# A transformer layer's first stage: deriving the combined weights inside the product loop, and moving row statistics to ScalarE

## What is computed

```python
xn = _layernorm(x, axis=-1)                       # (x - mean) / sqrt(var + 1e-5)
qkv = einsum('bsc,cf->bsf', xn, Wqkv) + bqkv      # 3 x 512 columns
attn = softmax(q @ k.T / sqrt(512)) @ v;  attn = attn @ Wo + bo
q_r = einsum('bsd,rd->bsr', xn, Wq_w)             # router, 16 columns
scores = einsum('bsr,er->bse', q_r, keys)         # 64 experts, the top 16 kept, softmax over them
z = einsum('bsd,nd->bsn', xn, A_w) * gate         # 512 columns
x = x + attn + einsum('bsn,on->bso', z, B_w) * 2
```

## Time and profile before

| | |
|---|---|
| Time, median of 3 runs | 2958.62 us (2958.13 to 2960.61) |
| Profiled execution: its own time, span | 2959.48 us, 2957.6 us |
| PE, PEld busy, share of the span | 94%, 76% |
| DVE, ACT, POOL busy | 63%, 32%, 25% |
| Mean granted PE clock | 0.983 |
| Phase A, groups 0 to 3: first matmul of the group at | 41.4, 442.6, 779.2, 1114.7 us |

### The profile page before, as it was taken

One profiled execution on the slowest core, in us unless ns is written; L12 is line 12 of the kernel. 1 busy time (PEld: TensorE's weight loads), 2 busy tenths in 40 slices (PEclk: granted clock), 3 DMA queues, 4 the chain that ended last, 5 costly groups with the idle time before them and its releaser, 6 DMA issues.

```text
span 2957.6 us, 34124 instructions
## 1 busy us (share of the span) xinstructions
PE 2772.5 (94%) x12096; PEld 2249.8 (76%) x12096; DVE 1858.8 (63%) x2133; ACT 931.8 (32%) x1164; POOL 736.4 (25%) x429
## 2 busy tenths in 40 slices
PE   2888999999999999999889999999999999999999
PEld 1666787878778787888668788787887878878787
DVE  5876777666776777364466655666556665566653
ACT  1222232323232223322244333343433434334331
POOL 7165212030120203020030502305033050330521
PEclk8999999999999999999999999999999999999999
DMA  9767455544554454333533534535445353453544
GB/s 371 232 234 237 153 192 166 183 138 152 187 180 142 163 177 137 115 99 107 180 105 121 174 131 137 178 121 174 130 136 177 122 176 128 136 176 124 175 143 136
DMA packets 261611, 476.34 MB, mean 161 GB/s; under 512 B 26864, under 2 KB 76016, under 8 KB 257264
## 3 DMA queue, kind: packets, MB, share of 16 engines
q1 hardware_dynamic: 223408, 372.45, 39.0%
q10 hardware_dynamic: 29376, 68.72, 6.6%
q0 software_dynamic: 8704, 33.56, 3.2%
HBM read 390.74 MB, written 83.91 MB: 160 GB/s over the span
## 4 chain that ended last, share of the span: by engine, by line
PE 74%; DVE 11%; DMA 4%; issue 4%; ACT 3%; SPq 2%; POOL 2%; DVEq 0%; ACTq 0%; POOLq 0%
PE psum L689 31%; PE psum L1448 13%; PE psum L1450 13%; PE psum L1449 13%; DVE prob L1645 3%; DVE w_lo L739 2%; PE psum L626 2%; DVE r_lo L1617 1%; ACT r_hi L1338 1%; SPq L362 1%; DVE s_lo L744 1%; DVE part L726 1%; DMA t_scratch<-xb 1%; DMA w_raw<-t_scratch 1%; DMA xb<-W_blocks 1%
## 5 line engine op out<-in xcount | busy, mean ns | idle before, releaser
L739 DVE TENSOR_TENSOR w_lo<-w_raw,w_hi 128x1024 fp32r<-128x1024 f32 x224 | 325.7, 1454 | 417.0 <-ACT w_hi L442 416.6
L442 ACT ACTIVATE w_hi<-w_raw 128x1024 fp32r<-128x1024 f32 x224 | 237.4, 1060 | 946.4 <-PE psum L689 812.7
L1617 DVE TENSOR_TENSOR r_lo<-r_raw,r_hi 128x1024 fp32r<-128x1024 f32 x256 | 380.3, 1500 | 189.4 <-ACT r_hi L1338 189.4
L1448 PE MATMUL psum<-r_hi,f_hi 128*128 128x512 f32 x1024 | 405.7, 396 | 30.4 <-DVE r_lo L1617 29.0
L1449 PE MATMUL psum<-r_lo,f_hi 128*128 128x512 f32 x1024 | 400.8, 391 | 0.0
L1450 PE MATMUL psum<-r_hi,f_lo 128*128 128x512 f32 x1024 | 400.6, 391 | 0.0
L689 PE MATMUL psum<-s_hi,w_hi 128*128 128x512 f32 x896 | 356.3, 398 | 40.8 <-DVE w_lo L739 27.6
L1583 POOL TENSOR_TENSOR res<-res,b_out 128x512 f32<-128x512 f32 x128 | 222.8, 1769 | 661.4 <-DMA res<-x 661.4
L689 PE MATMUL psum<-w_hi,s_hi 128*128 128x512 f32 x896 | 353.8, 395 | 32.5 <-DVE w_lo L739 32.4
L689 PE MATMUL psum<-s_lo,w_hi 128*128 128x512 f32 x896 | 352.9, 394 | 0.0
L689 PE MATMUL psum<-s_hi,w_lo 128*128 128x512 f32 x896 | 352.5, 393 | 0.0
(11 more groups left out here) (133 smaller groups left out, 4287.0 us busy)
## 6 DMA issues: line engine op xcount, KB each, us to landing
w_raw<-t_scratch SPq DMA_DIRECT2D x128, 512.0 KB, 3.9
w_raw<-W_blocks SPq DMA_DIRECT2D x96, 512.0 KB, 3.9
r_raw<-k_scratch SPq DMA_DIRECT2D x64, 512.0 KB, 3.8
r_raw<-v_scratch SPq DMA_DIRECT2D x64, 512.0 KB, 4.6
r_raw<-B_T SPq DMA_DIRECT2D x64, 512.0 KB, 3.9
res<-x SPq DMA_DIRECT2D x128, 256.0 KB, 4.9
r_raw<-Wo SPq DMA_DIRECT2D x64, 512.0 KB, 4.5
out<-res SPq DMA_DIRECT2D x128, 256.0 KB, 3.4
```

The costliest lines, as they stand in the source:

```text
L442: nc.scalar.activation(w_hi[:, s % RAW], w_raw[:, s % RAW], ACT.Copy).then_inc(s_whi, 1)
L739: nc.vector.tensor_tensor(w_lo[:, s % RAW], w_raw[:, s % RAW], w_hi[:, s % RAW].bitcast(F32), ALU.subtract).then_inc(s_wlo, 1)
L1448: pe.matmul(bank, sh, mh, start=first, stop=False)
L1617: nc.vector.tensor_tensor(r_lo[:, slot, :], r_raw[:, slot, :], r_hi[:, slot, :].bitcast(F32), ALU.subtract).then_inc(b_lo, 1)
```

## The change

Five things change together, nearly all in the first group.

1. **Weight sums on the way.** `sums_t` and its 1 MB loads are gone. In products 2 to 5 of the first group, DVE subtracts right after it has split a step's weights (`sum_weights`): it takes the raw weights that lie in `w_raw` and one more block that POOL has loaded. b22 (the weights of product 2) less b12 gives t3; b21 less b11 (this subtraction on POOL, `less_b11`) less t3 gives t4; b21 less t4 gives t2; b22 less t2 gives t1. SP stores each 512 KB result to `t_scratch` behind its weight load, and the next product loads it from there. The extra blocks lie in four slots of x12's place (products 2 and 3), then in `rows`.
2. **Rows first.** At the start ACT issues the four row tiles and then x11; SP issues the constants, and holds the first two weight loads back until row tiles 1 and 3 have landed. x21 and x22 are loaded by POOL, after the first two pairs of x11 are split.
3. **Router weight in rows.** `WqT` is laid out on the host so that a partition's 256 values are contiguous (before: runs of 16). Its split moves ahead of the loop.
4. **Statistics of later tiles on ACT** (`moments`): two passes over 128 x 2048 with the sum as a second output (Identity, then Square with the mean as bias) and three operations on one column. This is for tiles 4, 6 and 7 of the first group, at (0,3), (0,5), (0,6), and for all tiles of the next group at the new `STATS_AT`. Tile 5 stays on DVE, at (0,4). `store_stats` moves from (0,5) to (0,7), `broadcast_stats` from (0,6) to (1,0).
5. **Normalisation.** The pairs of x21 and x22 are at (1,1) to (1,4), two in each step; before they were spread over (1,0) to (1,4). Those of the second group's x12 are at (4,3) to (4,6) instead of (4,1), (4,2), (4,3), (4,5).

```diff
+SUMMED = {2: "t3", 3: "t4", 4: "t2", 5: "t1"}
 BIAS = [[4, 5, 0, 1], [6, 7, 2, 3]]
-STATS_AT = [(1, 1), (1, 2), (1, 3), (1, 4), (2, 1), (2, 2), (2, 3), (3, 1)]
+STATS_AT = [(1, 1), (1, 2), (1, 5), (2, 1), (2, 2), (2, 3), (2, 5), (2, 6)]
...
+NORM1_AT = [(4, 3), (4, 4), (4, 5), (4, 6), (5, 1), (5, 2), (5, 3), (5, 5), (6, 1), (6, 2), (6, 3), (6, 6)]
+OWN_AT = {(0, 3): 4, (0, 5): 6, (0, 6): 7}
...
+    def t_tile(idx, s):
+
+        return x_pair(1, s % PART) if idx < 4 else row_tile(s)
+
+    def row_tile(s):
+        return rows[:, s % PART // 2, s % 2 * 2 * W:(s % 2 + 1) * 2 * W].rearrange("p (a w) -> p a w", w=W)
...
-            if static(g) and g == 0 and ORDER[idx][1] in W_SUM:
-                for h in (s * 2, s * 2 + 1):
-                    sp.wait_ge(s_tstore[t_slot(h)], 16 * t_uses(t_slot(h), h + 1))
+            if static(g) and g == 0:
+                i, k = (idx, s - RAW) if s >= RAW else (idx - 1, s - RAW + IPI)
+                if i in SUMMED:
+                    sp.wait_ge(s_tdiff, t_number(i, k))
+                if idx - 1 in SUMMED:
+                    sp.wait_ge(s_tstore[s % PART], 16 * t_uses(idx - 1, s))
             sp.dma_start(w_raw[:, s % RAW], w_source(idx, s)).then_inc(s_raw[s % RAW], 16)
...
-            sp.dma_start(wq_raw[:], WqT.rearrange("(k p) r -> p k r", p=P)).then_inc(s_const, 16)
+            sp.dma_start(wq_raw[:].rearrange("p k r -> p (k r)"), WqT).then_inc(s_const, 16)
...
+        constants()
+        sp.wait_ge(s_row0[1], 16)
         load_w(0, 0, 0)
-        for p in range(PART):
-            sp.dma_start(x_pair(0, p), xT[2 * p * P:(2 * p + 2) * P, 0:W].rearrange("(a p) t -> p a t", p=P)
-                         ).then_inc(s_x[0][p], 16)
+        sp.wait_ge(s_row0[HT - 1], 16)
         load_w(0, 0, 1)
...
+                    if static(g) and g == 0 and idx in SUMMED:
+                        sp.wait_ge(s_tdiff, t_number(idx, s))
+                        sp.dma_start(t_block(idx, s), t_tile(idx, s)).then_inc(s_tstore[s % PART], 16)
...
+        def moments(g, j):
+            tile = rows[:, j % 2, :]
+            col = slice(j, j + 1)
+            if static(g) and g == 0:
+                base, loads = max(j - HT - 1, 0) * STAT_STEPS, (j - HT) // 2 + 1
+            else:
+                base, loads = (g * NTOK - NTOK + len(OWN_AT) + j) * STAT_STEPS, g * HT - HT // 2 + j // 2 + 1
+            chain = Chain(act, s_moments, base)
+            act.wait_ge(s_rows[j % 2], 16 * loads)
+            chain.link(nc.scalar.activation(tile, tile, ACT.Identity, accum_out=total[:, col]))
+            chain.step(nc.scalar.activation(mv[:, 0, col], total[:, col], ACT.Copy, scale=1.0 / C))
+            chain.link(nc.scalar.activation(less_mean[:, col], total[:, col], ACT.Copy, scale=-1.0 / C))
+            chain.link(nc.scalar.activation(tile, tile, ACT.Square, bias=less_mean[:, col], accum_out=squares[:, col]))
+            chain.link(nc.scalar.activation(var[:, col], squares[:, col], ACT.Copy, scale=1.0 / C))
+            act.sem_inc(s_amv, 1)
...
+        for p in range(PART):
+            x_load(0, 0, p)
+        act.wait_ge(s_const, 64)
+        act.wait_ge(s_wq, 1)
+        nc.scalar.activation(wq[:, :, 0:RD], wq_raw[:], ACT.Copy).then_inc(s_wq, 1)
...
+                    if first and (idx, s) in OWN_AT:
+                        moments(0, OWN_AT[idx, s])
...
+                        if s == 6:
                             square_roots(2, slice(HT, NTOK))
-                            wait(act, s_tiles, HT)
-                            for p in range(PART):
-                                x_load(0, 3, p)
-                        if s == 5:
+                        if s == 7:
                             store_stats(0, 2, HT)
-                        if s == 6:
-                            broadcast_stats(0, 2, HT)
+                    if first and idx == 1 and s == 0:
+                        broadcast_stats(0, 2, HT)
...
+                        if (idx, s) in STATS_AT:
+                            j = STATS_AT.index((idx, s))
+                            moments(g + 1, j)
+                            if j + 2 < NTOK:
+                                rows_load(g + 1, j + 2)
...
+        def sum_weights(idx, s):
+            tile = t_tile(idx, s)
+            dve.wait_ge(s_tload[s % PART], 16 * (t_uses(idx, s) + 1))
+            if idx == 3:
+                dve.wait_ge(s_tsum, s + 1)
+            if idx == 2:
+                ins = nc.vector.tensor_tensor(tile, w_raw[:, s % RAW], tile, ALU.subtract)
+            else:
+                ins = nc.vector.tensor_tensor(tile, tile, w_raw[:, s % RAW], ALU.subtract)
+            ins.then_inc(s_tdiff, 1)
...
+                    after = (idx, s + 1) if s + 1 < IPI else (idx + 1, 0)
+                    if first and after[0] in SUMMED:
+                        sum_weights(*after)
...
-                        if s < HT:
-                            stats_of_tile(0, HT + s)
                         if s == 3:
                             norm_pair(0, 1, 0)
                         if s == 4:
-                            rstd_ready(NTOK, slice(HT, NTOK))
-                            norm_pair(0, 1, 1)
-                            rstd_finish(2, NTOK * TILE_STEPS + RSTD_STEPS, slice(HT, NTOK))
-                        if s in (5, 6):
+                            stats_of_tile(HT + 1)
+                        if 4 <= s <= 6:
                             norm_pair(0, 1, s - 3)
+                        if s == 6:
+                            dve.wait_ge(s_mv, HT + 1)
+                            rstd_ready(len(OWN_AT), slice(HT, NTOK))
+                        if s == 7:
+                            rstd_finish(2, (HT + 1) * TILE_STEPS + RSTD_STEPS, slice(HT, NTOK))
                     elif first and idx == 1:
-                        if s == 0:
-                            norm_pair(0, 2, 0)
-                        if 1 <= s <= 3:
+                        if 1 <= s <= 4:
+                            norm_pair(0, 2, s - 1)
...
-        def sums_t(h):
-            slot, p, k = t_slot(h), h // HK, h % HK
-            b = t_tile(slot)
-            b11, b12, b21, b22 = (b[:, i, :] for i in range(4))
-            pool.wait_ge(s_tload[slot], 16 * t_uses(slot, h + 1))
-            nc.gpsimd.tensor_tensor(b11, b12, b11, ALU.subtract).then_inc(s_tadd, 1)
-            pool.wait_ge(s_tadd, 4 * h + 1)
-            nc.gpsimd.tensor_tensor(b12, b22, b12, ALU.subtract).then_inc(s_tadd, 1)
-            pool.wait_ge(s_tadd, 4 * h + 2)
-            nc.gpsimd.tensor_tensor(b22, b22, b11, ALU.subtract).then_inc(s_tadd, 1)
-            pool.wait_ge(s_tadd, 4 * h + 3)
-            nc.gpsimd.tensor_tensor(b21, b21, b22, ALU.subtract).then_inc(s_tadd, 1)
-            pool.wait_ge(s_tadd, 4 * h + 4)
-            pool.dma_start(t_scr[:, p, k * P:(k + 1) * P, :].rearrange("b p w -> p b w"), b
-                           ).then_inc(s_tstore[slot], 16)
...
+        def load_b12(s):
+            if s < PART:
+                pool.wait_ge(s_slo, pair(0, 2, s) + 1)
+            else:
+                stored(2, s - PART)
+            load_summand(2, s, "b12")
+
+        def load_b21_b11(s):
+            stored(2, PART + s) if s < PART else stored(3, s - PART)
+            load_summand(3, s, "b21")
+            if s < 2:
+                pool.wait_ge(s_amv, len(OWN_AT) + NTOK)
+            if s >= PART:
+                pool.wait_ge(s_tsum, s - PART + 1)
+            pool.dma_start(row_tile(s), w_block("b11", s // PART, s % PART)).then_inc(s_tload1[s % PART], 16)
+
+        def less_b11(s):
+            pool.wait_ge(s_tload[s % PART], 16 * (t_uses(3, s) + 1))
+            pool.wait_ge(s_tload1[s % PART], 16 * (s // PART + 2))
+            nc.gpsimd.tensor_tensor(t_tile(3, s), t_tile(3, s), row_tile(s), ALU.subtract).then_inc(s_tsum, 1)
+
+        def load_b21(s):
+            if s < PART:
+                pool.wait_ge(s_tsum, PART + s + 1)
+            else:
+                stored(4, s - PART)
+            load_summand(4, s, "b21")
+
+        def load_b22(s):
+            stored(4, PART + s) if s < PART else stored(5, s - PART)
+            load_summand(5, s, "b22")
...
+        pool.wait_ge(s_slo, 2)
+        for p in range(PART):
+            for block in (2, 3):
+                if block == 3:
+                    pool.wait_ge(s_tiles, HT)
+                pool.dma_start(x_pair(block, p), xT[((block % 2) * HK + 2 * p) * P:((block % 2) * HK + 2 * p + 2) * P, W:TG]
+                               .rearrange("(a p) t -> p a t", p=P)).then_inc((s_tload1, s_tload)[block - 2][p], 16)
         for p in range(PART):
             s3(0, p)
             s4(0, p)
-        sums_t(7)
-        load_t(9)
-        sums_t(8)
-        load_t(10)
-        sums_t(9)
-        load_t(11)
-        for h in range(10, T_ITEMS):
-            sums_t(h)
-            if h + 2 < T_ITEMS:
-                load_t(h + 2)
-        for p in range(PART):
-            s2_s1(0, p)
+        for s in range(IPI):
```

(13 more changed lines are left out.)

177 lines of the change are left out of this document (85 added, 92 removed).

## The result

The changed kernel takes 2951.12 us (median of 11; 2942.82 to 2955.75), the kernel before on the same chip 2960.61 (median of 11). The ratio is 0.9966, 95% interval 0.9956 to 0.9976: faster by 0.34%. The forecast was 2932, and its range ended at 2951. The sign was right and the size was a third of the forecast: 9.5 us instead of 27. The last digits of such a difference carry little: with no edit in groups 1 and 2, these two together took 1.6 to 3.6 us longer in every experiment's trace than in the changed kernel's.

What follows compares the result with a forecast made beforehand. PE's idle bounds it: about 118 us up to the end of product 4. Start and products 0 to 4 sum to 324.5 against 354.4, 29.9 less; less 0.8 and 2, 27.1 off 2959.5 gives 2932; range 2903 to 2951.

Steps and rivals of the forecast that it cites:

- Start, product 0: First matmul at 30 us instead of 41.4; product 0 takes 51 us, the 20.5 us wait for `wq` gone.
- the term of four tiles: Start: four row tiles of 3.3 us plus 0.8 for the router weight's split; the last starts at 15.7.
- ACT's statistics: Two passes of 2.0 us each, 5.0 a tile; groups 1 and 2 lose 2 us for both.
- rival 2: Crowded queues and slow ACT: 7 us a tile, 9 in all, product 2 stays at 52; 2945 to 2953; chance 0.18.
- Product 1: 84 us instead of 73.4: statistics in place at 21.4, then steps of 13.1 as DVE and POOL take turns.
- Product 3: 61 us, as now: 48 plus 13 for b11, the chain, the statistics store and queues; bounds 50 and 75.
- the wait for b11: Start of product 3: DVE stands for POOL's first b11 subtraction (9.5 us), delaying the split for (3,1); PE loses 3 us.
- the chain: Product 3: store landing, issues and subtractions bind each second tile, 11.5 us for two steps; costs 2 us.
- the store of the statistics: Product 3: the store at (3,4), landing in 10.2 us, holds up what is issued behind it; costs 6.6 us.
- Product 4: 50 us, 2 more than now: new subtraction and pair in (4,4), s2 and s1 turns in first three steps.
- Rival 3: Chain through HBM binds: landings of 11.0 us, 20 more in product 3, 15 in products 2, 4, 5; 2967; chance 0.06.
- Rival 1: Most idle goes (store lands in half the time or DVE and POOL overlap): 2907, 2893 at its end; chance 0.22.

Runs made afterwards that it cites:

- e9: Changed kernel with the router weight fetched in short runs as before, still first on SP's queue: 2965.37 us in one execution.
- e5: Changed kernel with POOL's block differences of product 1, first group, cut to 32 columns (outputs differ): 2936.49 us in one execution.
- e11: e8 with the x differences of product 1, first group, on DVE instead of POOL: 2929.17 us, ratio 0.9877.
- e7: e4 with three places on DVE reordered: subtraction of (3,0) behind drains, router copy of (3,3) earlier, x12 pairs one step later: 2948.42 us, ratio 0.9939.
- e6: e4 with group 1's statistics earlier on ACT and POOL's b11 subtraction ahead of its load for tile s+2: 2942.98 us, ratio 0.9920.
- e15: Changed kernel with only the eight subtractions of b11 moved from POOL to DVE: 2950.50 us in one execution.
- e14: Changed kernel with only POOL's arithmetic of the first group moved to DVE: 2932.78 us, ratio 0.9885.
- e4: Changed kernel with the broadcast of group 1's statistics issued at (4,0) instead of (3,5): 2950.22 us, ratio 0.9945.
- e16: e12 with the store of group 1's statistics in 32-byte instead of 4-byte runs (second group's statistics go to wrong tokens): 2912.56 us in one execution.
- e12: e11 with all of POOL's other arithmetic of the first group on DVE too: 2919.59 us, ratio 0.9844.
- e13: e12 with the store of group 1's statistics at (2,5) instead of (3,4): 2918.85 us, ratio 0.9842.
- e8: Changed kernel with the edits of e4, e6 and e7 together: 2937.65 us, ratio 0.9904.

## Why the prediction was right in sign and wrong in size

*Start, product 0: right.* First matmul at 31.2, no wait for `wq`, product 0 52.3. The second to fourth tiles come at DVE's pace (10.80, 13.97 and 17.14), as the term of four tiles assumed, and 14.1 us lie behind the last (forecast 14). e9 shows how much hangs on it: without the router weight in rows all is lost. It also corrects the reading of the earlier trace rows: the short runs hold SP 7.3 us by themselves, not 35.4.

*ACT's statistics: right.* The two passes take 1.9 and 2.01 us, and their accumulator reads 0.18 each, in all 4.7 a tile (forecast 5.0). Groups 1 and 2 moved by less than 0.5 us instead of 2. The first half of rival 2 (7 us a tile) is out, and so is its second: product 2 takes 45.4.

*Product 1: right in its steps, and by some luck in its sum.* Steps of 12.3 us (forecast 13.1). e5 and e11 confirm the turns in two independent ways: 62.7 us with POOL's part made small, 9.7 us a step with it on DVE. The rule of the Trainium skill (SBUF — State Buffer, section SBUF: two separate sides), that a DVE instruction with two SBUF inputs and a GpSimd one that reads SBUF exclude each other, is borne out. That (1,0) to (1,2) take 32.2 us, as forecast, is luck: the broadcast landed in 10.2 us, not 5.3, the store in 8.3, not 12.3, and the long pause came before (1,3), not before (1,2).

*Product 3: this step failed.* It read: "3 us of PE" for the wait for b11, "with the other work of DVE it costs 2" for the chain, 6.6 for the store of the statistics, 1.5 for queues: 13 in all. The steps measured 10.9 over the undisturbed at (3,0), 5.8 and 2.2 at (3,3) and (3,4), 7.9 and 2.7 at (3,6) and (3,7): 29.5. In detail:
- *(3,0), 10.9 instead of 3.* The wait for b11 was foreseen (9.5 in POOL's part; DVE stood 6.1). I asked what was behind it on DVE and named the split for (3,1). The drains of (2,7), which PE needs inside (3,0), were ahead of that split and I passed over them. That is not all: with the drains first (e7), (3,0) to (3,2) are still 6.2 over, twice the 3. What the runs show of the sources are late statistics and POOL's order (e6: 6.5 us together in (3,0), of which 2.5 come back in (2,7)) and POOL's arithmetic (e15: 3.4).
- *(3,3) and (3,4), 8.0 instead of the 2 for the chain.* I applied the turns at the port to product 1 and to s2 and s1, and for the eight subtractions of b11 only added their 2.35 to a chain. They too block DVE, two in a row for 6.29 us. With them on DVE (e14, e15) (3,3) takes 7.5.
- *(3,6) and (3,7), 10.6 instead of 6.6.* The landing of 10.2 was read off a trace in which DMA moved 218 GB/s; at 264 it was 18.7. Two edits remove it from different ends: e4 (ACT's wait) 8.7, and e16 (the pieces) 6.7 of what e12 had there.

*Product 4: 55.1 instead of 50.* The turns with s2 and s1 cost the first four steps nothing (5.4 us each); all of it is (4,4), 14.1 instead of 6.4. The new pair at (4,3), made longer by the turns with the last s2 and s1, stands ahead of the drains of (4,4), PE waits 5.2 us for them and then runs at a granted clock of 0.50 (319 to 322 us). With the pair behind them the step is 7.8 instead of 14.1 (e7), and on DVE alone the arithmetic gives 0.9 (e14).

*The rivals.* Rival 3 (the chain through HBM) is out as stated: landings of tiles and weights in products 2 and 4 were 5 to 7 us and those of the stores 6.5 and 7.8, not 10.2 to 11.0, and DVE never waited for a DMA of W_blocks. Rival 1, that the idle mostly goes, is what e13 and e16 reach by other edits. The time fell into rival 2's interval by none of its mechanisms. Its cost of "9 in all" is not what its own terms give (three times 7 less 3.3 is 11), and the 2893 of rival 1 is not worked out; neither enters the sum.

What stays open: why the product-3 steps vary between e8 and e11 with the same code there, and between changed, e5 and e9, beyond the store's landing; each has one trace.
